# A gated cross-attention and routed feed-forward kernel on one core: the scale and shift of the second norm travel with the rows

## The reference

```
x = x + tanh(g_xattn) * attention(layernorm(x), ctx)      # softmax(Q K^T) V / 16, one head, with biases
h = layernorm(x)                                          # "norm two"
e = argmax(h @ router_w.T)                                # one expert for each token
y = (silu(h @ gate_w[e].T) * (h @ up_w[e].T)) @ down_w[e].T
x = x + tanh(g_ffn) * y
```

## Time and profile before

| | |
|---|---|
| Median of 3 executions | 223.45 us (222.14 to 224.74) |
| The profiled execution | 221.01 us, of which the span of its instructions 218.9 us |
| Busy share of the span | PE 91%, weight loads 78%, DVE 60%, ACT 50%, POOL 62% |
| Chain that ended last | PE 83%, DVE 6%, ACT 3%, DMA 3%, issue 2% |
| Mean granted clock of PE | 0.96 of full speed |

### The profile page before, as it was taken

One profiled execution on the slowest core, in us unless ns is written; L12 is line 12 of the kernel. 1 busy time (PEld: TensorE's weight loads), 2 busy tenths in 40 slices (PEclk: granted clock), 3 DMA queues, 4 the chain that ended last, 5 costly groups with the idle time before them and its releaser, 6 DMA issues.

```text
span 218.9 us, 4538 instructions
## 1 busy us (share of the span) xinstructions
PE 199.7 (91%) x1200; PEld 170.9 (78%) x1200; DVE 130.8 (60%) x430; ACT 109.8 (50%) x223; POOL 136.1 (62%) x138
## 2 busy tenths in 40 slices
PE   7899999997665789999999999999999999999960
PEld 3667998985564678888888888888888888888850
DVE  2886899867699125537555537564636565645650
ACT  1478777664500534495269485369475444422410
POOL 3004099495473897339966998987998985212111
PEclk9999999999787589999999999999999999999996
DMA  6999315928600319621581085194003012011000
GB/s 208 340 394 378 135 49 163 368 73 291 217 0 0 99 25 358 211 68 38 189 313 32 0 311 189 34 383 126 1 8 92 0 51 68 9 49 51 5 28 20
DMA packets 11845, 29.43 MB, mean 134 GB/s; under 512 B 1986, under 2 KB 8517, under 8 KB 10790
## 3 DMA queue, kind: packets, MB, share of 16 engines
q1 hardware_dynamic: 6320, 20.20, 25.9%
q0 software_dynamic: 2064, 5.12, 7.8%
q10 hardware_dynamic: 3430, 3.74, 5.1%
HBM read 24.85 MB, written 4.72 MB: 135 GB/s over the span
## 4 chain that ended last, share of the span: by engine, by line
PE 83%; DVE 6%; ACT 3%; DMA 3%; issue 2%; ACTq 1%; POOL 0%; POOLq 0%; DVEq 0%
PE ps L929 36%; PE ps L941 12%; PE ps L908 6%; PE ps L944 5%; PE ps L790 3%; PE ps L729 3%; PE ps L770 3%; DMA both<-in_ctxT 3%; PE ps L811 3%; PE ps L759 2%; PE ps L901 2%; PE ps L800 2%; PE ps L750 2%; PE ps L878 1%; DVE V L1193 1%
## 5 line engine op out<-in xcount | busy, mean ns | idle before, releaser
L929 PE MATMUL ps<-wgu,xhT 128*128 x360 | 83.1, 384 | 1.2 <-DVE xhT L1229 1.2
L929 PEld LDWEIGHTS ps<-wgu,xhT 128*128 128x128 f32 x360 | 66.3, 191 | 12.5 <-issue 1.6
L464 POOL DMA_INDIRECT xin<-x_rows,table x23 | 22.7, 986 | 29.4 <-DVE xin L1264 21.5
L941 PE MATMUL ps<-wd,hT 128*128 x114 | 40.5, 392 | 0.0
L396 POOL TENSOR_TENSOR wgu<-raw_gu,wgu (+1 forms) x12 | 38.6, 3253 | 0.1
L1246 DVE TENSOR_TENSOR A<-xin,ps 128x512 f32<-128x512 f32 (+1 forms) x40 | 20.6, 520 | 25.4 <-ACT xin L656 14.6
L656 ACT ACTIVATE xin<-ps 128x512 f32<-128x512 f32 (+1 forms) x40 | 18.6, 465 | 31.5 <-PE ps L929 31.1
L469 POOL DMA_INDIRECT out<-xin,table x20 | 20.3, 1015 | 18.3 <-DVE xin L1264 13.2
L650 ACT ACTIVATE hT<-ps 128x512 fp32r<-128x512 f32 x20 | 11.8, 592 | 32.9 <-PE ps L908 32.9
L944 PE MATMUL ps<-wd,hT 128*128 x95 | 26.6, 280 | 0.0
L941 PEld LDWEIGHTS ps<-wd,hT 128*128 128x128 f32 x114 | 21.3, 187 | 3.9
(11 more groups left out here) (163 smaller groups left out, 310.7 us busy)
## 6 DMA issues: line engine op xcount, KB each, us to landing
raw_gu<-in_Wgu SPq DMA_DIRECT2D x8, 1408.0 KB, 6.5
both<-in_Wd SPq DMA_DIRECT2D x8, 640.0 KB, 4.3
x_rows<-x ACTq DMA_DIRECT2D x8, 256.0 KB, 3.4
xin<-in_x SPq DMA_DIRECT2D x7, 256.0 KB, 8.8
both<-in_WdL SPq DMA_DIRECT2D x16, 64.0 KB, 4.7
both<-in_ctxT ACTq DMA_DIRECT2D x2, 480.0 KB, 7.1
xin<-x_rows,table POOLq DMA_INDIRECT x23, 3.6
out<-xin,table POOLq DMA_INDIRECT x20, 2.7
```

What stands on the lines that cost most here:

```text
L464: pool.indirect_dma_start(out=xg[:, j % SEATS, :], out_offset=None, in_=rows, in_offset=bass.IndirectOffsetOnAxis(ap=table[:, j:j + 1], ax ...
L929: last = pe.matmul(ps[:, g, 0:2 * WIDE if g < 2 else 4 * REST], xhT[:, j % 2, x_part, c, :], w, start=(c == 0 and (x_part, w_part) == (0, 0)),
L941: last = pe.matmul(ps[:, 6, 0:2 * H], hT[:, 0, c, :], wd[:, slot, c].rearrange("p o a n -> p (o a n)"), start=(c == 0), stop=(c == CI - 1) ...
```

## The change

- x1 is written in place into `xin`, whose rows get two more columns (258 instead of 256): scale and shift of norm two. POOL computes them in two groups, `scales2(FIRST)` (6 of 16 token tiles) between the low pieces of expert 0 and expert 1, and `scales2(LATER)` (10) behind those of expert 1, guess included. The DRAM rows are 1032 bytes. SP sends them in two DMAs, the first 6 tiles and the spare row after arrived_d(1), the other 10 after load_d(2); ACT sends none. A gathered row brings its own scale and shift, so `r3`, `rsel`, `stat` and their matmuls (L891) go.
- The first context half is loaded in two parts of 240 KB, one on SP behind x of batch 0, one on ACT ahead of x of batch 1. PE waits for both.
- PE: 12 useless matmuls of 256 columns for the 5 of 512, 6 more ahead of `score_weights(0)`. `turn3(7)` goes ahead of `logits(6)`, and the last batch has its own x1T buffer and PSUM bank. `spin(8)` ahead of the ranks, 52 for 64 behind them, 2 in front of each of 12 table matmuls, 60 for 24 behind the table, 12 ahead of the first `up`.
- Routing: the count chain has 5 linked DVE instructions for 7; the high one-hot comes first and table matmuls follow the low one-hots one by one. DVE makes 12 low one-hots; ACT makes 4, by Square and Relu, and one factor of the table (`uv[:, :, 1, :]`). The past-count reduction is one instruction.

```diff
@@ sync
+            sp.dma_start(ctx_sb[:, 0, early], ctxT[0:P, early]).then_inc(d_ctx[0], 16)
             sp.dma_start(wv[:], ap(Wv, C)).then_inc(d_wv, 16)
...
                 arrived_gu(e)
                 if e:
                     load_d(e)
+                if e == SPLIT - 1:
+                    sp.wait_ge(p_st2, 2)
+                    sp.dma_start(rn[:, LATER], xin[:, LATER, :]).then_inc(d_row, 16)
                 arrived_d(e)
+                if e == 1:
+                    sp.wait_ge(p_st2, 1)
+                    sp.dma_start(rn[:, FIRST], xin[:, FIRST, :]).then_inc(d_row, 16)
+                    sp.dma_start(rows[N:N + 1, :], xin[0:1, 0, :]).then_inc(d_zrow, 16)
                 if e < SPLIT:
                     load_gu(e + RAW)
@@ gpsimd
-            for e in range(SPLIT - 1):
-                low_pieces(e)
-            pool.wait_ge(v_guess, 1)
-            link(newton(pool, link, mv2[:, :, 0], rs2[:, 0, :], rs2[:, 1, :], ALL))
...
+            def scales2(t):
+                pool.wait_ge(v_aggr, t.stop // TB)
+                link(guess(pool, link, mv2[:, t, 1], t))
+                newton(pool, link, mv2[:, t, 0], xin[:, t, H], xin[:, t, H + 1], t).then_inc(p_st2, 1)
+            low_pieces(0)
+            scales2(FIRST)
+            low_pieces(1)
+            scales2(LATER)
+            pool.wait_ge(d_row, 32)
             pool.wait_ge(d_zrow, 16)
             pool.wait_ge(v_tab, 1)
@@ scalar
-            act.dma_start(xin[:, TB:2 * TB, :], x[1].rearrange("(t p) h -> p t h", p=P)).then_inc(d_x[1], 16)
+            act.dma_start(ctx_sb[:, 1, early], ctxT[P:2 * P, early]).then_inc(d_ctx[0], 16)
+            act.dma_start(xin[:, TB:2 * TB, 0:H], x[1].rearrange("(t p) h -> p t h", p=P)).then_inc(d_x[1], 16)
...
+            act.wait_ge(v_slot, 1)
+            for t in range(SHARE):
+                if t == SHARE // 2:
+                    act.wait_ge(v_hi, 1)
+                    act.activation(uv[:, :, 1, :], ohhi[:], ACT.Copy, scale=iota_p[:, 0:1]).then_inc(a_uv, 1)
+                ins = act.activation(far[:, t, :], iota_lo[:], ACT.Square, scale=-1.0, bias=slot_f[:, 0, t:t + 1])
+            ins.then_inc(a_far, 1)
+            act.wait_ge(a_far, 1)
+            act.activation(ohlo[:, 0:SHARE, :], far[:], ACT.Relu, scale=-1.0, bias=one[:, 0:1]).then_inc(a_lo, 1)
@@ tensor
+            filler(12)
...
+            filler(6)
             score_weights(0)
...
+                if i == B - 1:
+                    turn3(i)
                 if i:
                     logits(i - 1)
...
+            pe.wait_ge(a_x1T, B)
+            spin(8)
             pe.wait_ge(v_sort, 1)
...
-            spin(64)
-            pe.wait_ge(v_lo, 1)
-            pe.wait_ge(p_lo, 1)
+            spin(52)
+            pe.wait_ge(v_uv, 1)
+            pe.wait_ge(a_uv, 1)
+            for n, t in enumerate(list(range(SHARE, NTOK)) + list(range(SHARE))):
+                if t >= SHARE:
+                    pe.wait_ge(v_lo, t - SHARE + 1)
+                    spin(2)
+                else:
+                    pe.wait_ge(a_lo, 1)
...
-            spin(24)
+            spin(60)
@@ vector
-            link(dve.tensor_scalar(n_of, ps[:, 0, NTOK * E:(NTOK + 1) * E], 1.0, float(P - 1), ALU.max, ALU.add))
-            link(dve.tensor_copy(cnt_i[:, 0, :], n_of))
-            link(dve.tensor_scalar(cnt_i[:, 1, :], cnt_i[:, 0, :], 7, 7, ALU.logical_shift_right, ALU.logical_shift_left))
-            link(dve.tensor_copy(padded, cnt_i[:, 1, :]))
-            link(dve.memset(cnt[:, 4, :], 0.0))
+            link(dve.tensor_scalar(n_of, ps[:, 0, NTOK * E:(NTOK + 1) * E], 1.0, 1.0 / P, ALU.max, ALU.mult))
+            link(dve.tensor_scalar(cnt[:, 3, :], n_of, 255.0 / 512.0, BIG, ALU.add, ALU.add))
+            link(dve.tensor_scalar(padded, cnt[:, 3, :], -BIG, float(P), ALU.add, ALU.mult))
```

More of the change, by code:

```diff
@@ L58 @@
 NORM = H ** -0.5
+FIRST, LATER = slice(0, 3 * TB), slice(3 * TB, NTOK)
+BIG = float(2 ** 23)
 def flamingo_moe(nc, x, ctxT, g_x, g_f, WqT, WkT, Wv, bv, WrT, Wgu, Wd, WdL, out):
@@ L133, in flamingo_moe @@
         turn = sb("turn", [P, NT], I32)
-        r3 = sb("r3", [P, NTOK, 3, 2], BF16)
-        stat = sb("stat", [P, 2, NT])
+        one = sb("one", [P, 1])
         table = sb("table", [P, NT], I32)
@@ L159, in flamingo_moe @@
         uv, _ = part(free_c[:, at:at + NTOK * NT].bitcast(BF16), 0, NTOK, 2, NT)
-        rsel, _ = part(V[:].rearrange("p b h -> p (b h)")[:, 0:NTOK * 3 * NT].bitcast(BF16), 0, NTOK, 6, NT)
+        far, _ = part(V[:].rearrange("p b h -> p (b h)").bitcast(BF16), 0, SHARE, P)
         mean_w = V[:, B - 1, 0:P]
@@ L168, in flamingo_moe @@
         rk, at = part(free_q, at, NTOK, E)
-        xg, at = part(free_x, 0, SEATS, H)
+        xg, at = part(free_x, 0, SEATS, HR)
         og, at = part(free_x, at, RING, H)
@@ L178, in flamingo_moe, with scale_of, shift_of @@
         exf, at = part(free_a, at, NT)
[L179 to L180 removed]
+        trf, at = part(free_a, at, NT)
         def seat(j):
[L184 removed]
+            return xg[:, j % SEATS, 0:H]
+        def scale_of(j):
+            return xg[:, j % SEATS, H:H + 1]
+        def shift_of(j):
+            return xg[:, j % SEATS, H + 1:HR]
         ps = stack.enter_context(nc.psum_tensor("ps", [P, 8, 512], F32))
@@ L372, in _ @@
                 lambda: pool.memset(mean_w, 1.0 / H),
+                lambda: pool.memset(one[:], 1.0),
             ]
@@ L568, in turned3 @@
                 act.wait_ge(t_t3, i + 1)
-                if i:
+                if 0 < i < B - 1:
                     act.wait_ge(t_lg, i)
-                act.activation(x1T, ps[:, 1, :].rearrange("p (c s) -> p c s", c=C), ACT.Copy).then_inc(a_x1T, 1)
+                act.activation(x1T if i < B - 1 else last_x1T, ps[:, 1, :].rearrange("p (c s) -> p c s", c=C), ACT.Copy).then_inc(a_x1T, 1)
             def high(src, dst):
@@ L622, in _ @@
                     split_first(i)
-            act.wait_ge(v_x1, B)
-            act.dma_start(rv[B - 1], x1[:, (B - 1) % 2]).then_inc(d_row[(B - 1) % 2], 16)
-            act.dma_start(rows[N:N + 1, :], x1[0:1, (B - 1) % 2, 0, :]).then_inc(d_zrow, 16)
             turned3(B - 1)
-            for step in range(B - 1, 3 * SPLIT):
+            split_first(B - 1)
+            act.wait_ge(v_slot, 1)
[7 more added lines that the diff above has]
+            act.activation(ohlo[:, 0:SHARE, :], far[:], ACT.Relu, scale=-1.0, bias=one[:, 0:1]).then_inc(a_lo, 1)
+            for step in range(B, 3 * SPLIT):
                 split_first(step)
@@ L694, in tile @@
                     silu(j, 1)
-            act.wait_ge(v_stat, 1)
-            act.wait_ge(v_exp, 1)
             gathered(0)
@@ L700, in _ @@
             gathered(1)
+            act.wait_ge(v_exp, 1)
             def drain(j):
@@ L712, in _, with filler @@
             pe.wait_ge(v_quiet, 1)
-            for _ in range(5):
-                pe.matmul(ps[:, 7, 0:2 * H], quiet[:, 0:P], quiet[:], start=True, stop=True)
+            def filler(n):
+                for _ in range(n):
+                    pe.matmul(ps[:, 7, 0:2 * P], quiet[:, 0:P], quiet[:, 0:2 * P], start=True, stop=True)
+            filler(12)
             for c in range(C):
@@ L810, in logits @@
                     for c in range(C):
-                        last = pe.matmul(ps[:, 5, E * k:E * k + E], x1T[:, c, P * k:P * k + P], wrc[:, c, :],
+                        last = pe.matmul(ps[:, LG_BANK(i), E * k:E * k + E], src[:, c, P * k:P * k + P], wrc[:, c, :],
                                          start=(c == 0), stop=(c == C - 1))
@@ L860, in _, with spin @@
                     router_mean()
-            turn3(B - 1)
             logits(B - 1)
+            def spin(n):
+                for _ in range(n):
+                    pe.matmul(ps[:, 1, 0:P], ones_b[:], tri[:], start=True, stop=True)
+            pe.wait_ge(a_x1T, B)
+            spin(8)
             pe.wait_ge(v_sort, 1)
@@ L873, in _ @@
             last.then_inc(t_rk, 1)
-            def spin(n):
-                for _ in range(n):
-                    pe.matmul(ps[:, 1, 0:P], ones_b[:], tri[:], start=True, stop=True)
-            spin(64)
-            pe.wait_ge(v_lo, 1)
-            pe.wait_ge(p_lo, 1)
-            for t in range(NTOK):
+            spin(52)
[7 more added lines that the diff above has]
+                    pe.wait_ge(a_lo, 1)
                 last = pe.matmul(ps[:, 2, 0:2 * NT], ohlo[:, t, :], uv[:, t].rearrange("p a n -> p (a n)"),
-                                 start=(t == 0), stop=(t == NTOK - 1))
+                                 start=(n == 0), stop=(n == NTOK - 1))
             last.then_inc(t_tab, 1)
-            for t in range(NTOK):
-                if t % (NTOK // 2) == 0:
-                    pe.wait_ge(v_rsel, 2 * t // NTOK + 1)
-                last = pe.matmul(ps[:, 3, 0:6 * NT], ohlo[:, t, :], rsel[:, t].rearrange("p a n -> p (a n)"), start=(t == 0), stop=(t == NTOK - 1))
-            last.then_inc(t_stat, 1)
-            spin(24)
+            spin(60)
```

(7 more changed lines are left out.)

131 lines of the change are left out of this document (49 added, 82 removed).

## The result

The changed kernel takes **225.69 us** (median of 20, 224.27 to 228.07) against 223.5 for the kernel before (20 executions): ratio **1.0118**, 95% interval 1.0087 to 1.015. It is slower, where I forecast 223.0 and no change; the median lies 0.1 us above the range that I gave (219.8 to 225.6), and "slower by more than 1%" had a chance of 0.15. Its profiled execution took 227.27 us, 225.0 of it span; that of before took 221.01, less than any of its 20 timed ones (from 221.37 on), so the 6.1 us between the two spans are more than the change costs. Every ratio here is of the fast executions of both kernels, those within 1.5% of the fastest of the same kernel, so it can differ from the quotient of two medians, and where a profiled execution was a slow one only lengths of stages are read from it.

The account below looks back on a forecast made before the run. PE bounds the kernel, the loop gives nothing, so the first up's start and length count; terms +0.7 +1.8 +0.5 -0.7 -0.3 -0.4 -1.2 +0.3 -1.1 sum to -0.4, from 223.45 to 223.0 us, range 219.8 to 225.6.

Parts of the forecast that it names:

- Batches (+1.8): POOL's scales delay its low pieces of expert 1, then SP's load, ACT's sixth split piece and PE: 1.8 us later.
- Clock in the tail (+0.5): PE's pause before batch 7's values grows from 0.9 to 2.7 us; clock may fall: 0 to 1.3 us, 0.5 taken.
- Start (+0.7): x of batch 1 lands 0.8 us late behind 240 KB of context on ACT's queue, less 0.1 slack: +0.7 us.
- Tail order, counts, table: After the batches: turn3(7) ahead of logits(6) saves 0.7 us, shorter count chain 0.4, faster slots to table 1.2.
- Ranks (-0.3): Rank matmuls to DVE's first count: useless matmuls ahead may raise the clock, 0 to -0.6 us, -0.3 taken.
- Rows in DRAM (+0.3): SP's last row DMA, 1.32 MB, takes 6.3 us and ties with the table ahead of the gather: +0.3 us.
- Gather to first `up`: Table to gather 0.93 us, then 3.3 us until ACT works on it: unchanged.
- First `up` (-1.1): Loop's first up: useless matmuls behind the table may keep the clock up, 0 to -2.1 us, half taken.
- POOL's lateness not reaching PE: Rival, chance 0.28: scales fit POOL's idle time or ACT has slack; +1.8 and +0.5 go, giving 220.7 us.
- The row DMA: Rival, chance 0.10: the row DMA becomes the gather's last condition; 228.3 us if it lands after 12 us.
- Useless matmuls on the path: Rival, chance 0.07: at low clock they delay ranks and table by 1.3 us, first up stays 5.7: 225.4 us.
- the forecast's own: Main case, chance 0.55: gains given back at the start and on ACT; own range 221.0 to 225.2 us.

Follow-up runs that it names:

- a_ready: Changed kernel with SP raising gu_ready for expert 2 ahead of load_gu(3) instead of behind it; ratio 0.9946 to the kernel before.
- a_warm2: Changed kernel with 40 useless matmuls of 128 columns in PE's pause ahead of batch 7's values, wait for SP left in; ratio 1.0033.
- a_again: Changed kernel run once more, unedited; ratio 1.0246 to the kernel before.
- b_ctx: Kernel before with only the context's first half loaded in two parts as in the change; ratio 1.006.
- a_ctx_back: Changed kernel with the first context half loaded as before, whole on ACT's queue behind x of batch 1; ratio 1.0023.
- a_behind_ready: Changed kernel with gu_ready for expert 2 raised early and, on ACT's queue, x of batch 1 ahead of its context part; ratio 0.9908.
- b_pitch: Kernel before with two unused columns added to the SBUF rows of x (pitch 1032 bytes); ratio 1.0042.
- a_ctx_ready: Changed kernel with the context loaded as before and gu_ready for expert 2 raised early; ratio 0.9791.
- a_ctx_ready2: Second measurement of the changed kernel with context loaded as before and gu_ready for expert 2 raised early; ratio 0.9893.
- a_best5: Changed kernel with early gu_ready and x of batch 1 ahead of its context part on ACT's queue, five rounds; 218.94 us, ratio 0.9842.

## Why the prediction was wrong, step by step

The step that failed is the price of the clock in the tail: +0.5 in the sum, at most 1.3 by my bounds, 1.9 to 3.3 by the runs. The second is the start: +0.7, about 1.8 by the runs. The chain POOL, SP, ACT, PE was right.

**Batches (+1.8): right in place and size.** ACT's piece waited for SP, 1.3 to 1.6 us in every execution with the late raise, and PE's pause, where nothing filled it, grew by 1.4 to 1.7. The added lateness of ACT was 2.16 in the first pair. The rest comes from ahead of the scales: POOL began the low pieces of expert 0 at 32.42 for 27.70, 0.45 more than the start's 4.27. Its 16 instructions for the scales took 4.6 us, where I had counted 4.7. `a_ready` shows that it was this link.

**Clock in the tail (+0.5): this is the term that failed most.** I bounded it by 1.3 and took 0.5, counting the values and the transposes. The logits run slower too at 0.50 (1.71 and 1.85 for 1.06), and they and a copy between them are in series. With -0.7 for the order I had the tail 0.2 shorter; it was 2.4, 1.1 and 2.1 longer in the three kernels with an empty pause. Without the pause the new tail is worth -0.8, so the clock cost 1.9 to 3.3. `a_warm2` takes out 1.9 us with the wait still there. The pause of 0.9 to 2.7 us was seen and its danger named; what it would do was priced from the shortest reading of the rows behind it.

**Start (+0.7): mechanism right, size too small.** Between the classes of the table it is +1.8 at the first norm. I had the context landing early and only x of batch 1 late by 0.8. In the trace x of batch 0, whose place on SP's queue is unchanged, also came later (means 7.4 and 6.6 us over the same classes, which overlap), and the context was not early at all in the profile after. The Trainium skill ("DMA: Bandwidth & Descriptors", "Queues, rings and completion order") says that a DMA engine goes round the queues that have work, a packet at a time; that agrees with a load on ACT's queue holding up one on SP's, though no trace here shows the packets. And in the first profile the clock fell behind PE's wait for x (0.57 from 15.1 to 18.2), which I had priced nowhere. The length of the wait does not decide it: behind 2.35, 2.37 and 2.63 us it fell (after, a_again, a_warm2), behind 3.04 and 2.82 it did not (b_ctx, a_ready); what does is open. By time, `a_ctx_back` and `b_ctx` give 2.1 and 1.4 us for the whole of this edit. The profile that I read was also the earliest of nine at this point (10.24; the other eight 10.5 to 11.3). I took one execution for the rule; whether it was a good draw or the other eight are late by their pitch of 1032 bytes can't be told. Among the kernels with that pitch the parts ahead make the first norm 1.7 later (12.8 for 11.1), in the one pair without it 2.8 (13.08 for 10.24).

**Tail order, counts, table: right.** -0.8 for -0.7, -0.4 for -0.4, -1.3 for -1.2. ACT's part (Squares, copy, Relu) ended at 73.74 while DVE's low one-hots went on to 74.3, and no table load stood between 4.5 and 84 us.

**Ranks (-0.3): nothing,** 1.34 us for 1.33 at low clock, since the tail before them was already low. Where the clock was still up at the ranks they took 0.88 and 0.89 (a_ready, a_behind_ready).

**Rows in DRAM (+0.3): length right, price nil.** The 1290 KB landed 6.3 us after issue, at 72.7. (In the page's KB my sum is 3.4 + 3.1 x 1034 / 1152 = 6.2; I had mixed two units.) In this pair there was no tie: the table ended 2.7 us later, held back by the clock in the tail; and my end of the table had left out the +0.5. The tie came in `a_ready` and `a_behind_ready`, where the DMA is named as the last condition of the gather, yet the gather follows the table by the same 0.96 us.

**Gather to first `up` (unchanged): -0.4,** of which 0.25 lie between the first gather and ACT's work on it (3.02 for 3.27).

**First `up` (-1.1): -0.65 in the pair; a lottery.** From 5.02 to 6.60 with the change's useless matmuls, as the fall of the clock lies, and 5.01 to 6.61 in the three kernels without them (before, b_ctx, b_pitch).

**The rivals.** The first (POOL's lateness not reaching PE) fell with the trace. The row DMA fell. Useless matmuls on the path: the 52 behind the ranks ended at 72.0, 0.64 us ahead of the first table step. The case that came is the forecast's own with the clock lost twice. The rivals lacked a case, "a longer pause brings the clock down and all behind it runs at half": with the mean tail of the three kernels, +1.9 for my net -0.2, and 1.8 for the start's 0.7, the same sum, worked out after the fact, gives -0.4 + 2.1 + 1.1 = +2.8; 1.18% of 223.5 is 2.6. The smaller misses (ranks +0.3, first `up` +0.45, row DMA -0.3, gather -0.4) cancel.

**Not settled.** The weight of the 1032-byte pitch (`b_pitch` allows up to 2 us): the only profile of the old order without it is that of the kernel before, so a second profile of that kernel would be the test. Why that profile alone of 14 shows no dip of the DMA rate in the sixth microsecond (355 GB/s; the others 175 to 276). And what lets the clock fall behind one wait of PE and not behind a longer one.

## What to carry to other kernels

When an edit lengthens a pause of PE, make a case in which everything serial behind the pause runs at the lower clock, not only the first matmuls (it came in all three kernels with the empty pause in the tail, and behind three of five such waits at the start); or fill the pause, or remove the wait. A semaphore raised behind another wait on a queue's program makes a third engine wait for something that it doesn't need: raise it as soon as its own condition holds. A load that gates a long serial chain goes ahead of a bigger one that only one step needs, even where the bigger one is what PE is seen waiting for.

## What the runs showed of the hardware that was not expected

- x of batch 0, first behind the key weights on SP's queue, landed between 5.5 and 8.3 us over 14 profiles; with the same kernel (`after`, `a_again`) at 8.3 and 7.2. One profile of a start is one draw.
- Six waits of PE of 2.3 to 2.6 us (ahead of the first transposes in after, a_again and a_warm2, ahead of batch 7's values in after, a_again and a_ctx_back) saw the granted clock fall to 0.50, inside the wait or up to 1.5 us behind it; waits of 2.8 and 3.0 us at the start of a_ready and b_ctx left it at 1.00.
- The loop's step of 6.67 us was 7.0 to 7.9 us three or four times in four profiles of one chip (a_ctx_back, a_ready, a_ctx_ready, b_ctx), mostly with PE waiting for nothing that the profile shows, and once in a_ctx_ready2 and a_best5. Timeline of PE in `a_ctx_back`, transposes of two tiles 7.90 us apart:

```profile
186.10 0.82 PE L924 MATMUL ps<-ident,A 128*128 128x128 f32 x6
...
194.00 0.85 PE L924 MATMUL ps<-ident,A 128*128 128x128 f32 x6 [0.60 <-issue]
```

  They are in versions of both kernels and cost 2 to 3 us in each of the four, so they are no part of the change. The kernel before has no profile from that set; its median there was 226.2 us, and 223.6 on the same chip later.
